# Sixteen Z tiles on ScalarE, code products three tiles later, and weights behind the first codes, in the head of a two-layer graph kernel

## The reference

```
deg = max(rowsum(adj != 0), 1)
L0: pooled = D^-1/2 (adj + I) D^-1/2 x + x;   x = layernorm(x + relu(pooled @ W0 + b0))
L1: two products with adj of x; attention over the edges,
    e = exp(-leaky_relu(s_left[i] + s_right[j])) where adj != 0, normalised by its row sum;
    out = sigmoid(attn_a * (attn @ h) + attn_b * (adj @ (x @ Wg) + bg));  x = layernorm(x + out)
```

## Time and profile before

| | |
|---|---|
| Median of the three runs | 875.16 us |
| The profiled execution | 876.12 us |
| Its span | 874.3 us |
| TensorE busy | 855.1 us (98%) |
| VectorE, ScalarE, GpSimd busy | 667.5, 508.7, 225.3 us |
| DMA busy, first 13 of 40 slices | 9 tenths or more |

### The profile page before, as it was taken

How to read it: one execution, slowest core, us unless ns; L and a number is a source line. 1 busy time by engine, 2 the same in 40 slices (tenths; PEclk the granted TensorE clock), 3 DMA queues, 4 the chain that set the end, 5 groups by cost and what they waited for, 6 DMA issues and landing times.

```text
span 874.3 us, 20237 instructions
## 1 busy us (share of the span) xinstructions
PE 855.1 (98%) x7579; PEld 755.0 (86%) x7579; DVE 667.5 (76%) x1182; ACT 508.7 (58%) x1150; POOL 225.3 (26%) x245
## 2 busy tenths in 40 slices
PE   8899999999999998998999999999999999999997
PEld 7788888888888887887888888888888888888886
DVE  5676756665655568898988987988978978978863
ACT  4441322222222337988976876976966967867831
POOL 3603454444432221012022022032032032032031
PEclk9999999999999999999999999999999999999999
DMA  9999999999996333320330230230230330330001
GB/s 261 104 176 144 169 197 170 114 181 154 145 176 128 137 139 109 56 53 4 79 80 25 54 78 24 54 78 24 54 78 14 64 78 0 78 78 0 25 25 37
DMA packets 127928, 79.66 MB, mean 91 GB/s; under 512 B 69848, under 2 KB 126208, under 8 KB 126464
## 3 DMA queue, kind: packets, MB, share of 16 engines
q0 software_dynamic: 33792, 16.78, 23.7%
q1 hardware_dynamic: 85152, 53.75, 22.9%
q10 hardware_dynamic: 8928, 8.38, 3.1%
HBM read 99.87 MB, written 29.36 MB: 148 GB/s over the span
## 4 chain that ended last, share of the span: by engine, by line
PE 77%; issue 8%; DVE 5%; ACT 4%; POOL 3%; DMA 2%; SPq 0%; POOLq 0%; ACTq 0%; DVEq 0%
PE ps L1491 31%; PE ps L1327 21%; PE ps L1432 19%; PE ps L1362 4%; POOL codes L408 2%; ACT ec L588 2%; DMA xs<-in_x_dram 1%; DVE ec L1063 1%; ACT em L597 1%; PE ps L1347 1%; DVE em L1070 1%; DVE dd L904 0%; POOL zb L431 0%; DMA x1r<-x_scratch 0%; DVE sc L762 0%
## 5 line engine op out<-in xcount | busy, mean ns | idle before, releaser
L1491 PE MATMUL ps<-fb,em 128*128 128x257 f16 x3072 | 347.5, 273 | 0.8 <-DVE em L1070 0.8
L1491 PEld LDWEIGHTS ps<-fb,em 128*128 128x128 f16 x3072 | 300.5, 98 | 38.6 <-issue 1.3
L1327 PE MATMUL ps<-y,codes 128*128 128x257 f16 x2048 | 237.8, 273 | 2.0 <-DVE codes L755 1.7
L1327 PEld LDWEIGHTS ps<-y,codes 128*128 128x128 fp8e4 x2048 | 200.1, 98 | 28.9 <-issue 2.1
L588 ACT ACTIVATE ec<-slb,nsb 128x256 f32<-128x256 f32 x512 | 211.1, 496 | 0.5 <-issue 0.3
L1070 DVE SCALAR_TENSOR_TENSOR em<-ec,em 128x2048 f16<-128x2048 f32 x64 | 147.5, 2305 | 23.3 <-ACT em L597 23.1
L597 ACT ACTIVATE em<-ec 128x2048 f16<-128x2048 f32 x64 | 122.1, 1909 | 64.8 <-PE ps L1491 57.3
L1063 DVE SCALAR_TENSOR_TENSOR ec<-ec,pan 128x2048 f32<-128x2048 f32 x64 | 147.3, 2301 | 2.6 <-issue 1.8
L458 POOL TENSOR_TENSOR sc<-sc,sc 128x2 f32<-128x2 f32 x15 | 38.5, 2569 | 245.9 <-DVE sc L1172 245.9
L1432 PE MATMUL ps<-zz,dd 128*128 128x256 f16 x768 | 89.4, 273 | 1.5 <-DVE t L1092 1.3
L1432 PEld LDWEIGHTS ps<-zz,dd 128*128 128x128 fp8e4 x768 | 75.0, 98 | 10.7 <-issue 2.0
(11 more groups left out here) (154 smaller groups left out, 816.3 us busy)
## 6 DMA issues: line engine op xcount, KB each, us to landing
codes<-in_adj_dram POOLq DMA_DIRECT2D x64, 256.0 KB, 11.8
a_scratch<-codes SPq DMA_DIRECT2D x8, 2048.0 KB, 9.4
pan<-a_scratch SPq DMA_DIRECT2D x16, 1024.0 KB, 7.0
x_scratch<-x ACTq DMA_DIRECT2D x32, 128.0 KB, 5.2
x1r<-x_scratch SPq DMA_DIRECT2D x16, 256.0 KB, 2.7
h_scratch<-hst ACTq DMA_DIRECT2D x30, 136.0 KB, 5.2
out_dram<-ot SPq DMA_DIRECT2D x15, 256.0 KB, 2.2
fb<-h_scratch SPq DMA_DIRECT2D x3, 1088.0 KB, 8.8
```

The lines of the kernel that those rows point to most:

```text
L1327: mm = pe.matmul(ACC(n), codes[:, qq % SLOTS, jb, (2 * h + e) * P:(2 * h + e + 1) * P].bitcast(F8), y[:, jb, part, 0:YC], start=(jb == 0 a ...
L1491: mm = pe.matmul(PH(2 * m + e)[:, 0:HC], em[:, c, e_part, i, e * P:(e + 1) * P], fb[:, jb, h_part, 0:HC], start=(jb == 0 and e_part + h_pa ...
```

## The change

Five constants change, and one is new: 11 warming transposes for 20; ScalarE copies Z tiles 0 to 15 instead of 0 to 11; the code products follow the Z tiles by 16 steps instead of 13 (so the first stands behind Z tile 16, not 13); the two weight steps go from 16 to 20 and from 23 to 27. `y` tiles begin at step 16 instead of 12 and come two a step, instead of three in two steps. VectorE makes its `y_lo` tiles ahead of its Z copy instead of behind it. SyncE issues the ten weight transfers once chunk 0 of the codes has landed, instead of at once. VectorE's last group of codes in the head has five instead of three.

```
-ZACT = 12
-ZLAG = 13
+ZACT = 16
+ZLAG = 16
+YAT = 16
-WT_AT = 16
-WNORM_AT = 23
+WT_AT = 20
+WNORM_AT = 27
-WARM = 20
+WARM = 11
...
+            sp.wait_ge(codes_in[0], 16)
             load_weights()
...
-            upto = lambda i: 0 if i < ZACT else min(i - 1, 3 * (i - ZACT) // 2 + 2)
+            upto = lambda i: 0 if i < YAT else min(i - 1, 2 * (i - YAT) + 2)
...
             for t in range(ZACT, T):
+                for i in split_at(t):
+                    y_lo(i)
                 if t == WT_AT:
                     gate_columns()
                 if t == WNORM_AT:
                     weight_norm()
                 z_copy(t)
-                for i in split_at(t):
-                    y_lo(i)
...
-            code(3)
+            code(5)
```

## The result

The changed kernel takes 883.42 us (median of 5 runs, 881.87 to 884.29) against 875.16 (5 runs of before): a ratio of 1.0087, 95% interval 1.0074 to 1.0100. It is slower by 8.3 us; forecast were 882.1 us, 6.9 more than before. The profiled execution took 884.29 us, its span is 882.5 us: 8.2 more than the span of before.

The account below looks back on a forecast made before the run. TensorE, busy 98% of the span, was taken to bound the kernel. Sum: 7.85 (weights wait) - 2.9 - 0.8 + 0.7 + 2.1 (clock) = +6.95, giving 882.1 us; 8-in-10 range 875.5 to 884.6.

Parts of the forecast that it names:

- The weights land at 39.1: Weight transfers in the head: issued when chunk 0 lands at 22.5, ten take 16.6 us beside the codes.
- A wait of 7.85 us: TensorE at step 20 stands from 31.25 to 39.1 us for the weights, swallowing everything won before.
- The clock, 2.1: Behind the weights wait TensorE's clock falls to its lower level, costing 2.1 us, bounds 0 and 3.4.
- First code product at 25.35, 2.9 us won there: Head: first code product 0.36 us later than before but three Z tiles further on, 2.9 us won.
- x at 8.7 us: Start of head: tile 4's transposes start at 8.7 instead of 10.02, paced by x, winning 1.3 us.
- this case with up to 1.2 us: Start of head: if the clock rises one stretch later, up to 1.2 us of gain goes, sum unchanged.
- Small waits, 0.8 won and 0.7 lost: Rest of the head: three small TensorE waits go (0.8 us); about 0.7 us is new at the norm.
- the reason for the second: At the norm: a pair of y_lo (0.87 us) ahead of VectorE's reduce causes the new 0.7 us.
- Weights in time: Rival, chance 0.13: the codes' backlog doesn't delay the weights, the head wins 2.7 us, 872.5 us.
- A shorter wait with the clock held: Rival, chance 0.13: weights land at 35 to 37 us, clock does not fall, 875.9 to 877.9 us.
- 2.07 us sufficed at 413 to 415 us: Argument against a held clock: after that TensorE wait before the change, 3.4 us ran at the lower level.
- Codes no sooner: Rival, chance 0.06: chunk 0 still lands at 24.4, weights at 41, 1.9 us more, 884.0 us.

Follow-up runs that it names:

- e4: Changed kernel with the last two weight transfers (512 B each) on their own semaphore, so TensorE waits only for the other eight: 878.30 us, ratio 1.0013.
- e3: Changed kernel with 64 idle transposes of the identity ahead of TensorE's wait for the weights: 881.36 us, ratio 1.0059.
- e9: Kernel of e6 with chunk 0's codes ahead of the y_lo pair at step 16 and Z copy ahead of y_lo from step 17: 872.96 us.
- e8: Changed kernel with 20 warming transposes instead of 11: 882.85 us, ratio 1.0083.
- e1: Changed kernel without its wait for chunk 0 ahead of the weight transfers, which go out at once: 873.83 us, ratio 0.9971.
- e5: Changed kernel with the weight transfers split, five issued by SyncE and five by ScalarE, both after chunk 0: 876.69 us, ratio 1.0014.
- e2: Kernel before with one edit, the weight transfers going out once chunk 0 of the codes has landed: 887.62 us, ratio 1.0129.
- e6: Kernel of e1 with y tiles begun at step 14 and chunk 0's codes ahead of VectorE's copy of Z 16: 873.72 us, ratio 0.9979.

## Why the prediction was right

The direction, the place and the two mechanisms were right, and the time within 1.3 us. By its own steps (the profiled executions, 8.2 us apart):

- *The weights land at 39.1.* Measured 39.7, from two errors that cancel, so that it came out so near is in part luck: chunk 0 landed at 20.5, not 22.5 (2.0 sooner), and the ten transfers took 19.2 us from the first issue, not 16.6 (2.6 longer). The turns were priced right (123 packets a us, as in the sum); what was not is the end of the queue, 196 packets in 4.7 us, and e4 shows its price: 3.2 to 3.3 us.
- *A wait of 7.85 us.* Measured 7.21. From the restart, 10.7 us later than the same transpose before, and with four more Z tiles (4.34) and one more code step (0.88) done ahead of it, the net is 5.5.
- *The clock, 2.1.* Measured 2.6 in the profile (45.35 instead of 42.8 for tile 22's transposes), 2.1 to 2.6 by e3.
- *First code product at 25.35, 2.9 us won there.* This is the step that failed: it began at 26.46, and 1.8 were won. I let x at 8.7 us hide the half rate at the start; but in this execution x's transposes and the first Z product ran at 1.2 GHz until past 7 us (5.29 2.07 above), and tile 4 began at 9.57. The prediction had this case with up to 1.2 us. In e3 and e9, with the same start of the head, tile 4 began at 8.72 and 8.68 as drawn, and the first code product of e3 at 25.66: so some 0.9 of the 1.1 us is the execution's own, and the sum was 0.2 to 0.3 short for VectorE's chain. It changed nothing, since the wait for the weights took it up; e8 shows that, and in e1 it decides what is won.
- *Small waits, 0.8 won and 0.7 lost.* Measured 0.8 and 0.6; the reason for the second was wrong (e9). In the terms of the sum the profiles give 7.21 - 1.8 - 0.8 + 0.6 + 2.6 = 7.8, where 6.95 was forecast.
- *The rivals.* Weights in time: e1 shows what that would have been, 873.8 (forecast 872.5). A shorter wait with the clock held: e5 comes near it. In e4 the weights were in at 35.9 and the wait was 3.9 us, and the clock fell all the same. But the reason given against this rival, that 2.07 us sufficed at 413 to 415 us, holds of that execution only: behind the same wait the clock held in four of the eleven profiles (the last point of this document has rows). Codes no sooner: they came 3.9 us sooner.

The other 0.4 of the 8.2 us lie in the second layer: one wait of TensorE for VectorE is 2.51 us instead of 2.07. It is 2.42 to 2.51 in all kernels with the new head and 2.07 in e2, so it comes with the new head and not with the late weights; the cause is open.

The Trainium skill ("DMA: Bandwidth & Descriptors", Latency and other measured facts) gives some 0.6 us to a first byte; here q1's first packet came more than 3.4 us after the issue (none from 20.52 to 24), with the codes' queue at its full 417 packets in 2 us. The same page (Queues, rings and completion order) says that an engine goes round the queues with work, a packet at a time; the pairs of rows from 26 to 31 us and e5's three queues agree.

## What to carry to other kernels

Before a transfer is moved behind another stream, count its packets and not its bytes: against a full queue ten weight transfers of 1 MB in 1550 packets needed 19 us from issue to landing. But count the later issue first: in the kernel before the same transfers, behind x in their queue, needed 15 us too (issued from 8.74, q1's last packet before 23.5), with 5 to spare before TensorE came for them at 29.01. They now land 16 us later, 12 of it because they go out at 20.52 and 4 because they take longer. Find the first instruction that needs the last of them, and take the time from the landing, not from the work ahead of it: gains ahead of such a wait are lost. And a wait of some microseconds on TensorE can cost twice, once as a wait and once as half rate behind it; where it can't be removed, idle matmuls in it save the second part (e3).

## What the runs showed of the hardware

- A codes queue that shares the engines with another starts later: in the changed kernel q0 sent 537 packets from 17 to 20 us, 407 of them at its full rate from 18 on, where the kernel before had none until 18 and 157 from 18 to 20, though GpSimd had issued the first of them at the same time (14.5 and 14.6 us). This is the 3.9 us that chunk 0 won. No computing engine could use them, as VectorE came to the chunk only at 25.9; what they did is let the weights go out sooner.
- A queue's last packets can dribble: 85 in 2 us at the end of q1 in the changed kernel, all of 4 B, where packets of 512 B went at 144 a us. The engines are not slow with packets of 4 B as such: in e5, from 31 to 32 us, ScalarE's queue sent 119 of them while the other two queues sent as many big ones:

```profile
q0 software_dynamic: 123, 0.06, 69.0%
q1 hardware_dynamic: 119, 0.11, 41.0%
q10 hardware_dynamic: 119, 0.01, 8.8%
```

From 36 to 38 us of the changed kernel q0 sent 284 beside q1's 85. With turns packet for packet that would fit a few DMA engines that still had packets of q1 and others that had none; which, no run shows.
- TensorE's clock fell inside waits of 7.2 us (2.4 us into it), 5.9 (e8) and 11.9 (e2). With one of 3.9 us (e4) it fell 0.8 us after TensorE had started again. It held with one of 1.3 (e3) and one of 0.8 (e5). Behind the wait of 2.07 to 2.51 us in the second layer it fell in seven of the eleven profiled executions and held in four (e2, e5, e6, e9). The 2.07 us of the kernel before are among the seven, the 2.07 us of e2 among the four. Here are e1 and e6, both behind 2.42 us, with 32 products at either level:

```profile
414.07 5.38 PE L1433 MATMUL ps<-fa,pan 128*128 128x260 f16 x32 [2.42 <-DVE s L1102]
...
413.42 3.71 PE L1437 MATMUL ps<-fa,pan 128*128 128x260 f16 x32 [2.42 <-DVE s L1106]
```
